# A vision block on one core: attention matmuls moved to 64x32 array tiles, score groups of four and two, value sums in two banks

## What is computed

```python
h = _L0_tok_ref(x, W, b, cls)                       # (4, 3137, 128)
q, k, v = (split_heads(_layernorm(h) @ w) for w in (Wq, Wk, Wv))
attn = einsum('bhsd,bhtd->bhst', q, k) * scale + pos_bias
attn = softmax(attn, axis=-1)
out = einsum('bhst,bhtd->bhsd', attn, v)
h = h + merge_heads(out) @ Wo
y = _layernorm(h)                                   # per image: softmax pooling, top-2 gate
h = h + sum over the two picked experts e of g[b, e] * gelu(gelu(y @ w1[e] + b1) @ w2[e] + b2)
```

## Time and profile before

| | us |
|---|---|
| median of 3 runs | 3004.4 (3003.92 to 3008.26) |
| the profiled execution | 3005.91 |
| its span, first to last instruction | 3004.3 |
| of it the attention exponentials, first to last start | 209.8 to 2613.9 |

### The profile page before, as it was taken

The page is one execution under the profiler, slowest core; times in us unless marked ns, Lnnn a source line. Parts: engine busy times, 40 slices in busy tenths (PEclk is TensorE's granted clock), DMA queues, the critical chain, the costliest instruction groups (busy, mean ns, idle before and its releaser), DMA issues.

```text
span 3004.3 us, 53203 instructions
## 1 busy us (share of the span) xinstructions
PE 2819.5 (94%) x21844; PEld 955.0 (32%) x21844; DVE 805.6 (27%) x1182; ACT 2574.9 (86%) x2422; POOL 779.8 (26%) x1421
## 2 busy tenths in 40 slices
PE   7989999999998999999989999999999999999997
PEld 3442222222222222222222222222222222355554
DVE  5751111111122324111222332111323232134411
ACT  4669999999998999999989999999989999844553
POOL 2123222222223233222233332223323223200000
PEclk9989999999999999999999999999999999999999
DMA  5540000000100000011010000101000001121010
GB/s 144 167 146 21 29 28 26 26 26 29 37 26 29 31 26 26 26 47 37 26 31 29 27 26 24 44 31 38 28 18 29 23 24 44 52 87 33 17 33 19
DMA packets 65626, 120.92 MB, mean 40 GB/s; under 512 B 10034, under 2 KB 55180, under 8 KB 63892
## 3 DMA queue, kind: packets, MB, share of 16 engines
q1 hardware_dynamic: 63324, 110.93, 11.7%
q0 software_dynamic: 2048, 6.43, 0.6%
HBM read 67.30 MB, written 51.30 MB: 39 GB/s over the span
## 4 chain that ended last, share of the span: by engine, by line
PE 43%; ACT 34%; issue 16%; DMA 4%; DVE 1%; SPq 1%; POOL 0%; ACTq 0%; POOLq 0%
ACT shared L824 34%; PE ps L738 16%; PE ps L664 6%; PE ps L707 6%; PE ps L715 6%; PE ps L661 5%; PE ps L691 3%; DMA halves<-att_rows 2%; DMA k_halves<-halves 1%; PE ps L607 1%; DVE std L939 0%; PE ps L601 0%; PE ps L622 0%; DMA band_rows<-band_sb 0%; SPq L455 0%
## 5 line engine op out<-in xcount | busy, mean ns | idle before, releaser
L824 ACT ACTIVATE shared<-ps 128x1572 f32<-128x1572 f32 (+1 forms) x1857 | 2256.3, 1322 | 140.4 <-PE ps L661 61.3
L738 PE MATMUL ps<-shared,va 128*32 128x393 f32 x12800 | 1448.2, 528 | 0.2 <-DVE flag_i L971 0.2
L900 POOL TENSOR_TENSOR shared<-shared,e_all 128x310 f32<-128x310 f32 (+19 forms) x1344 | 722.2, 550 | 1691.4 <-ACT shared L824 1686.2
L664 PE MATMUL ps<-qa,ka 48*128 48x393 f16 (+12 forms) x3808 | 634.2, 320 | 52.6 <-ACT shared L824 49.9
L661 PE MATMUL ps<-qa,ka 51*128 51x393 f16 (+18 forms) x3360 | 573.1, 316 | 59.1 <-ACT shared L824 54.7
L738 PEld LDWEIGHTS ps<-shared,va 128*32 128x32 f32 x12800 | 360.5, 149 | 499.4 <-issue 406.8
L664 PEld LDWEIGHTS ps<-qa,ka 48*128 48x128 f16 x3808 | 185.6, 95 | 585.9 <-ACT shared L824 437.2
L661 PEld LDWEIGHTS ps<-qa,ka 51*128 51x128 f16 (+1 forms) x3360 | 155.5, 95 | 619.0 <-ACT shared L824 518.0
L977 DVE COPY xc<-ps 128x393 f32<-128x393 f32 x64 | 36.4, 569 | 1168.3 <-PE ps L738 1168.3
L842 ACT ACTIVATE qa<-ps,b 128x393 f32<-128x393 f32 x256 | 136.5, 586 | 82.6 <-PE ps L707 82.6
L982 DVE RECIPROCAL sq<-sq 128x393 f32<-128x393 f32 x64 | 167.4, 2615 | 2.2
(11 more groups left out here) (137 smaller groups left out, 1344.1 us busy)
## 6 DMA issues: line engine op xcount, KB each, us to landing
qa<-q_halves SPq DMA_DIRECT2D x64, 196.5 KB
ka<-k_halves SPq DMA_DIRECT2D x64, 196.5 KB
att_rows<-std SPq DMA_DIRECT2D x64, 196.5 KB, 2.6
v_rows<-v_sb SPq DMA_DIRECT2D x4, 1600.0 KB, 6.7
va<-v_rows SPq DMA_DIRECT2D x32, 200.0 KB, 16.0
ln_rows<-ln SPq DMA_DIRECT2D x32, 196.5 KB, 5.4
q_halves<-halves SPq DMA_DIRECT2D x32, 196.5 KB, 3.0
k_halves<-halves SPq DMA_DIRECT2D x32, 196.5 KB, 3.9
```

The costliest lines, as they stand in the source:

```text
L664: last = nc.tensor.matmul(out[:, cut:W], ka[r:r + 48, par, k0:k0 + keys], qa[r:r + 48, par, q0 + cut:q0 + W], start=True, stop=True, tile_ ...
L738: last = nc.tensor.matmul(ps[quad:quad + 32, O_PS, 0:W], va[0:keys, par, :, kt], pr[0:keys, g % SLOTS_PR, j], start=(kt == 0), stop=(kt == ...
L824: nc.scalar.activation(pr[:, g % SLOTS_PR, 0:m], ps[:, b0:b0 + m, 0:W], ACT.Exp, scale=1.0 / (LIFT * LIFT)).then_inc(s_exp, 1)
L900: nc.gpsimd.tensor_tensor(p, p, e_all[0:keys, n % HEADS, t:t + z - a], ALU.mult).then_inc(s_biased, 1)
```

## The change

- Scores: each unit is cut into four tiles of 64 rows x 32 columns (three for the last key tile, the third with a single key), each with its own weight load and matmul. The row half goes by the unit's number (r = 64 * (u % 2)).
- Values: each unit's 128 keys are cut into two halves of 64; the low half uses array rows 0 to 63 and sums in bank 6, the high half rows 64 to 127 and bank 7. So all attention matmuls have one tile shape, 64x32.
- Groups: 4 and 2 units, banks 0 to 3 and 4 to 5. Guests stay in bank 3 of the group of four.
- Order: at most one batch follows `scores(g)`, and none follows a guest, unless a batch is at least HOLD = 5 groups back.
- Drain: VectorE copies bank 6 when the low half is done (`s_pv_low`), then adds bank 7 when the high half is done. The next pass's low half waits for the copy, its high half for the add.
- Around it: the ones in `va` are written so that keys past the end are zero; `pr` no longer fills all of `shared`; TensorE waits for the last drain before the expert stage, whose guests use bank 6.

```diff
-        size = GMAX - len(groups) % 2
+        size = GMAX - 2 * (len(groups) % 2)
@@ scores
-                        r = 64 * (j % 2)
+                        r = 64 * (u % 2)
-                        if cut > 0:
-                            last = nc.tensor.matmul(out[:, 0:cut], ka[r:r + 51, par, k0:k0 + keys], qa[r:r + 51, par, q0:q0 + cut],
-                                                    start=True, stop=True, tile_position=(r, 0))
...
+                        for x in range(0, keys, 32):
+                            y = min(x + 32, keys)
+                            if cut > 0:
+                                last = nc.tensor.matmul(out[x:y, 0:cut], ka[r:r + 51, par, k0 + x:k0 + y], qa[r:r + 51, par, q0:q0 + cut],
+                                                        start=True, stop=True, tile_position=(r, x))
...
@@ values
-                        pe.wait_ge(s_o, at(m // KT))
-                    for u in batches[m]:
...
+                    for half in range(2):
+                        r = 64 * half
+                        if kt == 0 and m > 0:
+                            if half == 0:
+                                pe.wait_ge(s_o_low, m // KT)
+                            else:
+                                pe.wait_ge(s_o, at(m // KT))
+                        for u in batches[m]:
...
+                            last = nc.tensor.matmul(ps[quad:quad + 32, O_PS + half, 0:W], va[r:r + 64, par, :, kt], pr[r:r + 64, g % SLOTS_PR, j],
+                                                    start=(kt == 0), stop=(kt == KT - 1), tile_position=(r, quad))
+                        if half == 0 and kt == KT - 1:
+                            last.then_inc(s_pv_low, 1)
@@ the loop of TensorE
+                    turn = 1
                     if g in guest_at:
-                        visit(guest_at[g], GUEST_PS)
-                    while done < NB and group_of[batches[done][-1]] + (done % KT == 0) <= g - DELAY - AHEAD:
+                        visit(guest_at[g], GMAX - 1)
+                        turn = 0
+                    while done < NB:
+                        lag = g - group_of[batches[done][-1]] - (done % KT == 0)
+                        if lag < DELAY + AHEAD or (turn == 0 and lag < HOLD):
+                            break
                         values(done)
                         done += 1
+                        turn = 0
+                pe.wait_ge(s_o, at(2 * NBH))
@@ drain
-                    dve.wait_ge(s_pv, BATCHES + KT * (q + 1))
-                    nc.vector.tensor_copy(o_sb[:, side], ps[:, O_PS, 0:W]).then_inc(s_o, 1)
+                    dve.wait_ge(s_pv_low, q + 1)
+                    nc.vector.tensor_copy(o_sb[:, side], ps[:, O_PS, 0:W]).then_inc(s_o_low, 1)
+                    dve.wait_ge(s_o_low, q + 1)
+                    dve.wait_ge(s_pv, BATCHES + KT * (q + 1))
+                    nc.vector.tensor_tensor(o_sb[:, side], ps[:, O_PS + 1, 0:W], o_sb[:, side], ALU.add).then_inc(s_o, 1)
```

More of the change, by code:

```diff
@@ L31 @@
 SLOTS_PR = 8
+HOLD = 5
 BATCHES = 100
@@ L180, in build @@
             xt = shared[0:50].rearrange("p (b t) -> p b t", b=B)
-            pr = shared[:].rearrange("p (g j w) -> p g j w", g=SLOTS_PR, j=GMAX)
+            pr = shared[:, 0:SLOTS_PR * GMAX * W].rearrange("p (g j w) -> p g j w", g=SLOTS_PR, j=GMAX)
             w_emb = sbuf(ctx, "w_emb", [50, P])
@@ L329, in build @@
             s_o = primed(held, "f_o")
+            s_o_low = semaphore(held, "f_o_low")
+            s_pv_low = semaphore(held, "f_pv_low")
             s_shuf = semaphore(held, "f_shuf")
@@ L365, in build @@
                       s_norm_mm, s_norm, s_v_mm, s_v, s_band_mm, s_right, s_shift, s_band, s_hid, s_hid_mm, s_eo, s_eo_mm]
-            GUEST_PS, LATE_PS, HID_PS, EO_PS = 3, 6, 0, 4
+            LATE_PS, HID_PS, EO_PS = 6, 0, 4
             GUESTS = 4 * CH + 1
@@ L388, in build @@
             LATE[LATE_GATE] = B * GUESTS - 1
-            O_PS = 7
+            O_PS = 6
             NLD = 10
@@ L500, in _ @@
                         if (b, c) == (2, 0):
-                            sp.wait_ge(s_init, 3)
+                            sp.wait_ge(s_init, 6)
                             sp.wait_ge(s_v_out[0], 16)
@@ L657, in scores @@
                         cut = min(max(k0 - REACH - q0, 0), W)
-                        r = 64 * (j % 2)
+                        r = 64 * (u % 2)
                         out = ps[0:keys, GMAX * (g % 2) + j]
-                        if cut > 0:
-                            last = nc.tensor.matmul(out[:, 0:cut], ka[r:r + 51, par, k0:k0 + keys], qa[r:r + 51, par, q0:q0 + cut],
-                                                    start=True, stop=True, tile_position=(r, 0))
-                        if cut < W:
-                            last = nc.tensor.matmul(out[:, cut:W], ka[r:r + 48, par, k0:k0 + keys], qa[r:r + 48, par, q0 + cut:q0 + W],
-                                                    start=True, stop=True, tile_position=(r, 0))
+                        for x in range(0, keys, 32):
[3 more added lines that the diff above has]
+                                                        start=True, stop=True, tile_position=(r, x))
+                            if cut < W:
+                                last = nc.tensor.matmul(out[x:y, cut:W], ka[r:r + 48, par, k0 + x:k0 + y], qa[r:r + 48, par, q0 + cut:q0 + W],
+                                                        start=True, stop=True, tile_position=(r, x))
                     last.then_inc(s_score, 1)
@@ L731, in values @@
                         pe.wait_ge(s_vld[par], (n // 2 + 1) * 16)
-                        pe.wait_ge(s_o, at(m // KT))
-                    for u in batches[m]:
[L734 to L739, removed]
+                    for half in range(2):
[6 more added lines that the diff above has]
+                        for u in batches[m]:
+                            n, kt, c = units[u]
+                            quad = 32 * (c % 4)
+                            g, j = place(u)
+                            last = nc.tensor.matmul(ps[quad:quad + 32, O_PS + half, 0:W], va[r:r + 64, par, :, kt], pr[r:r + 64, g % SLOTS_PR, j],
+                                                    start=(kt == 0), stop=(kt == KT - 1), tile_position=(r, quad))
+                        if half == 0 and kt == KT - 1:
+                            last.then_inc(s_pv_low, 1)
@@ L740, in values @@
                     last.then_inc(s_pv, 1)
                 done = 0
-                for g in range(NG + DELAY + 2):
+                for g in range(NG + DELAY + AHEAD):
                     if g < NG:
                         scores(g)
+                    turn = 1
                     if g in guest_at:
-                        visit(guest_at[g], GUEST_PS)
-                    while done < NB and group_of[batches[done][-1]] + (done % KT == 0) <= g - DELAY - AHEAD:
+                        visit(guest_at[g], GMAX - 1)
[4 more added lines that the diff above has]
+                            break
@@ L869, in _ @@
                 pool.wait_ge(s_init, 2)
-                nc.gpsimd.memset(va[:, :, HD:32], 1.0).then_inc(s_init, 1)
+                nc.gpsimd.memset(va[:, :, HD:32, 0:KT - 1], 1.0).then_inc(s_init, 1)
                 pool.wait_ge(s_init, 3)
+                nc.gpsimd.memset(va[64:P, :, HD:32, KT - 1], 0.0).then_inc(s_init, 1)
+                pool.wait_ge(s_init, 4)
+                nc.gpsimd.memset(va[0:64, :, HD:32, KT - 1], 1.0).then_inc(s_init, 1)
+                pool.wait_ge(s_init, 5)
+                nc.gpsimd.memset(va[64:LAST, :, HD:32, KT - 1], 1.0).then_inc(s_init, 1)
+                pool.wait_ge(s_init, 6)
                 def step(b, s):
@@ L1084, in _ @@
                     if g in guest_at:
-                        receive(guest_at[g], GUEST_PS)
+                        receive(guest_at[g], GMAX - 1)
                     if g in drain_at:
```

## The result

The changed kernel takes 2964.4 us (median of 4 runs, 2959.3 to 2965.8) against 3006.3 (4 runs, 3003.9 to 3012.0) for the kernel before on the same chip: a ratio of 0.9855, 95% interval 0.9836 to 0.9874. The forecast was 2966, faster. The profiled execution spans 2963.2 us, 41.1 less than before.

The account below looks back on a forecast made before the run. ScalarE's stream of exponentials was taken as the bound. The stage's terms, 2198 + 59 + 54 + 10 + 24 + 20, made 2365 us against 2404; with 1 for the end, the kernel goes from 3004.3 to 2966 us, range 2925 to 3055.

Parts of the forecast that it names:

- streaming: ScalarE's exponentials in groups of 4 and 2, 3 at guests, stream in 2198 us, 12 more than now.
- loop through the banks: Scores wait for the exponential two groups back: 2.12 us against 2.06 streamed per pair, 59 us in all (20 to 100).
- 99 guests: ScalarE's stalls at guests in the attention stage: 0.55 us each, 54 us, half of today's (20 to 110).
- DMA waits: Three guests that wait for a DMA: about 24 us of stalls stay.
- ends of passes: Stalls where a pass's values drain and batches catch up: 10 us where some 50 stand now.
- clock dips: Stretches of the attention stage at the lower granted clock: about 20 dips, 20 us, stay.
- Bound: ScalarE's stream of exponentials sets the attention stage's pace: 0.33 us per unit and some 0.04 per instruction.
- TensorE's own work: One tile shape removes shape-change costs; 12 units need 3.2 us against 4.24 of the loop, 1 us to spare.
- rival (b): Eight tiles don't stream side by side: a batch takes 1.37 us, TensorE is the bound, kernel 3460 us; chance 0.08.
- Rival (a): The loop eats the gain: 0.10 us late per pair, guests keep 0.8 us, kernel 3030 us; chance 0.15.
- Rival (c): TensorE's issue of 54,000 weight load and matmul pairs becomes the bound, from 0.044 us a pair on; chance 0.07.

Follow-up runs that it names:

- e5: Changed kernel with groups of 3 and 3 units instead of 4 and 2: 2889.6 us, ratio 0.9614 to the kernel before.
- e1: Kernel before with the new order rule alone, its own groups, tiles and one value bank kept: 2956.6 us, ratio 0.9839.
- e2: Changed kernel with the old order rule, batches also right after a guest: 3022.7 us, ratio 1.0056 to the kernel before.
- e4: Kernel before with groups of 4 and 2 alone: 3113.3 us, ratio 1.0353.
- e7: Kernel before with its own tiles and one value bank, plus the new order rule and groups of 3 and 3: 3086.8 us, ratio 1.0265.
- e9: Kernel before with its own tiles and one value bank, plus the new order rule and groups of 4 and 2: 3090.2 us, ratio 1.0292.
- e3: Changed kernel with scores in 64x128 tiles again, values staying in 64x32: 3109.7 us, ratio 1.0351 to the kernel before.
- e6: Changed kernel with each score matmul cut in two along its columns: 3191.5 us, ratio 1.0608 to the kernel before.
- e8: Changed kernel where a pass's first batch waits once, for both halves' addition, instead of once per half: 2961.5 us, ratio 0.9853 to the kernel before.
- e10: Changed kernel with each score matmul cut in three along its columns: 3920.5 us, ratio 1.3054 to the kernel before.

## Why the prediction was right, point by point

| term, us | predicted | measured |
|---|---|---|
| streaming | 2198 | 2206 |
| loop through the banks | 59 (20 to 100) | 58.5 |
| 99 guests | 54 (20 to 110) | 56.3 |
| DMA waits | 24 | 22.6 |
| ends of passes and clock dips | 10 + 20 | 18 |
| stage | 2365 | 2361.6 |

The row of pass ends and dips is what the others leave of the stage. That the sum is right within 4 us is in part luck: the stream was put 8 us too low and the last row 12 too high. The range doesn't follow from the terms either. The two bounds that are given, 20 to 100 for the loop and 20 to 110 for the guests, make 2893 to 3063, not 2925 to 3055.

- **Bound.** ScalarE's stream still paces the stage. The fit gives 0.051 us for an instruction instead of "some 0.04", and 0.3275 instead of 0.33 for a unit, 8 us in the sum.
- **Loop.** The mechanism is as predicted; the equal sums flatter it, as 13 of the 58.5 us are the steps of 17 ns behind groups of four, and the 59 stood for all 984 pairs, the 58.5 for those away from guests. Over short windows of ScalarE, two exponentials of four, and the load between them:

```profile
501.54 1.48 ACT L843 ACTIVATE shared<-ps 128x1572 f32<-128x1572 f32 x1
...
503.07 0.11 PEld L666 LDWEIGHTS ps<-qa,ka 51*32 51x32 f16 x6 [1.30 <-ACT shared L843]
...
503.68 1.49 ACT L843 ACTIVATE shared<-ps 128x1572 f32<-128x1572 f32 x1
```

  Done at 503.02, loads at 503.07, next start at 503.68: 1.48 + 0.05 + 0.61 = 2.14, where the prediction had 2.12 (its third part was 0.55, and 0.04 for the last tile). Over the whole stage the medians are 1.481, 0.050 and 0.604, together 2.135, and that is also the median time from one group of four to the next (1.378 + 0.757). The weight loads behind the 0.04 are of bf16 in the earlier trace rows, not of fp16; the fp16 loads of 32 columns take 0.090. e5 shows what the loop costs by removing it.
- **TensorE's own work.** "With one shape both go" is what the traces show: 0.67 from batch to scores (0.83 before), no gap behind the scores. Eight tiles stream side by side, against rival (b).
- **Guests.** The two steps were put at 0.1 and 0.4 us, though the sum took 0.55 for both; the medians are 0.13 behind the guest group and 0.29 behind the next, and smaller ones behind them and a few large ones make up the rest. The price of today was put at 80 to 110; 112.7 is a little above. e1 and e2 show from both sides that the place of the batch is the cause.
- **Ends of passes.** Of 46.5 us in units 10 to 29 of a pass, 18.0 are left, and 14.6 of these are the even loss of the text above, 51 and 17 ns a group; some 3 us for what was put at 10. 22.3 of the 46.5 were clock dips, which the next point takes up.
- **Clock.** This term was wrong: some 20 us of dips were said to stay. The gaps between exponentials that begin in such stretches hold 29.7 us of excess before and 7.8 after. The stage has 18 stretches at the lower level before, 6 after. Before, 12 of the 18 lie at units 10 to 19 of a pass, behind the wait for the copy of the one value bank, as in the earlier trace rows; 3 lie at the guests that wait for a DMA and 3 at units 87 to 94. After, just these last two kinds are left. At units 10 to 19 there are 10 in e1, 12 in e4, 12 in e7 and 8 in e9, all with one value bank; none in e2, e3, e5, e6 and e8, with two. (e10, with two, has 10 there among 38 in all, but its TensorE pauses everywhere.) So these dips belong to the end of a pass, and should have gone with it. Whether the second bank or the 64x32 value tiles do it, no run separates.
- **Rival (a)** fell on both its conditions: 0.07 us per pair instead of 0.10, and guests that did improve. **Rival (c)** has a real limit behind it, 0.030 us per pair, but under its break-even of 0.044; the changed kernel needs a pair each 0.042 us (9498 in 400 us). The Trainium skill's figure of about 62 ns per matmul ("TensorE: Matmul & The Clock Gate", section "Step-by-step: what each phase is for"), which it gives for decoding in software, does not hold for this kernel by these rows. Its other figure, a floor of about 25 ns from start to start (section "Wait — 56ns, not 53.3ns?"), is near the measured mean of 30, but here single matmuls in different tiles start closer together: the 8 of one round of a batch in the changed kernel start within 0.05 us.

What the prediction did not see is that the parts work against each other. It gave the groups' cost as the loop's 59 us and the tiles' use as spare time on TensorE; measured, the groups cost 134 us with the old tiles and the tiles give 126 back. And it did not ask whether the gain at the guests could be had alone (2956.6), nor whether other groups fit the new tiles better (2889.6). So the forecast of the whole came true, but the tiles and the groups, most of the change, had no part in its gain over e1.

## What to carry to other kernels

When matmuls of two tile shapes alternate, giving them one shape can be worth more than it looks; but group sizes must be chosen again with it, by the loop from one use of a bank to the next, not only by the streaming time. When a change bundles an order rule with new tiles, price the parts alone: here the cheap one had the whole gain, and the rest added nothing until the groups were evened out. Before cutting matmuls into more pieces, count load and matmul pairs per microsecond and stay clearly below what the engine is supplied with.

## What the runs showed of the hardware beyond that

Weight loads of the changed kernel, a run of 8 in the timeline, and the group of all of L669:

```profile
500.90 0.11 PEld L669 LDWEIGHTS ps<-qa,ka 48*32 48x32 f16 x8 [1.00 <-ACT shared L843]
...
L669 PEld LDWEIGHTS ps<-qa,ka 48*32 48x32 f16 x15200 | 244.4, 90 | 609.2 <-ACT shared L843 524.9
```

- TensorE was supplied with one instruction per 15 ns as a lasting rate (e10), in packets of 16 KB each 3.75 us, behind whose arrival it goes on after pauses, while bursts are much faster: the 8 loads here are over in 0.11 us at 0.09 each, so they start within 0.02.
- The fp16 load of 48x32 takes 0.090 us on the mean, that of 48x128 0.095: a quarter of the columns saves 5 ns.
- A change between 64x32 and 64x128 tiles costs TensorE 0.19 us behind a batch (0.86 in e3 against 0.67) and 0.11 behind the scores of a group of four (0.44 against 0.33), lost overlap included and taken as the difference of two kernels.
- ScalarE takes 1.360 or 1.377 us from the start of an undisturbed exponential of four units to the next start, and little between: 401 and 310 of 829 before, 8 and 949 of 984 after. What chooses between them is open.
